# Mamba's D skip: from two matmuls a unit on TensorE to a multiplication and an addition on GpSimd

## The reference, cut to what matters

```
zxbcdt = x @ in_w
z, xBC, dt = split(zxbcdt);  dt = softplus(dt + dt_bias)
xBC = silu(causal 4-tap convolution of xBC)
xs (4 heads x 64), Bm (128), Cm (128) = split(xBC)
y = ssd(xs * dt, dt * A, Bm, Cm)          # chunked state-space scan
y = y + D_skip[head] * xs                 # the D skip
y = y * silu(z)                           # the gate
y = y * rsqrt(mean(y*y) + 1e-5) * norm_w
out = y @ out_w
```

## Time and profile before

| what | us |
|---|---|
| median of 3 runs | 2361.59 |
| the runs | 2361.59, 2362.1, 2351.86 |
| the profiled execution, its own time | 2355.98 |
| span of the profiled execution | 2354.0 |
| outside the span | 1.98 |
| PE busy in the span | 1775.5 (75%) |
| DVE busy | 1386.8 (59%) |
| POOL busy | 993.7 (42%) |
| ACT busy | 821.7 (35%) |

### The profile page before, as it was taken

The page is one execution under the profiler, slowest core; times in us unless marked ns, Lnnn a source line. Parts: engine busy times, 40 slices in busy tenths (PEclk is TensorE's granted clock), DMA queues, the critical chain, the costliest instruction groups (busy, mean ns, idle before and its releaser), DMA issues. The chain is left out here.

```text
span 2354.0 us, 38902 instructions
## 1 busy us (share of the span) xinstructions
PE 1775.5 (75%) x11182; PEld 1463.1 (62%) x11183; DVE 1386.8 (59%) x3442; ACT 821.7 (35%) x1791; POOL 993.7 (42%) x1144
## 2 busy tenths in 40 slices
PE   3979833799999999999588993277772897357673
PEld 3559731488888888888445883166661465247663
DVE  4445465688888888885544445733446344843435
ACT  1322212455555555554132221033331322034331
POOL 2017540376666666665201652155551001045552
PEclk9999955899999999999599995588895767578887
DMA  6001120000000000000400115011112001201114
GB/s 192 1 10 42 36 73 0 0 2 1 1 2 1 1 2 1 1 1 1 156 0 10 37 37 156 8 37 38 38 37 74 1 0 59 58 27 39 39 37 125
DMA packets 60844, 81.39 MB, mean 35 GB/s; under 512 B 24720, under 2 KB 30896, under 8 KB 60720
## 3 DMA queue, kind: packets, MB, share of 16 engines
q1 hardware_dynamic: 46640, 51.01, 7.0%
q0 software_dynamic: 14080, 28.86, 4.4%
HBM read 54.93 MB, written 24.90 MB: 34 GB/s over the span
## 5 line engine op out<-in xcount | busy, mean ns | idle before, releaser
L650 POOL DMA_INDIRECT rows_in<-xn_rows,slot_token x220 | 221.0, 1004 | 461.4 <-SPq L643 395.6
L696 PE MATMUL ps<-w,inner_slot 128*128 x1760 | 269.3, 299 | 92.5 <-DVE y L787 64.5
L656 POOL DMA_INDIRECT y_rows<-y,slot_row x220 | 224.6, 1021 | 246.2 <-DVE y L787 138.3
L684 PE MATMUL ps<-gT,w_slot 128*128 128x128 f32 x1760 | 270.0, 303 | 52.9 <-ACT gT L718 48.3
L696 PEld LDWEIGHTS ps<-w,inner_slot 128*128 128x128 f32 x1760 | 239.6, 210 | 110.1 <-issue 109.6
L684 PEld LDWEIGHTS ps<-gT,w_slot 128*128 128x128 f32 x1760 | 245.0, 215 | 64.9 <-issue 42.7
L764 DVE TENSOR_TENSOR hb<-ps,b 128x512 f32<-128x512 f32 x142 | 98.1, 691 | 274.0 <-PE ps L684 135.1
L1431 DVE SCALAR_TENSOR_TENSOR cv<-ps,cw,cv 128x1021 f32<-128x1021 f32 (+2 forms) x192 | 245.1, 1277 | 17.6 <-ACT cv L1369 15.1
L1529 POOL TENSOR_TENSOR y<-t,sz 128x256 f32<-128x256 f32 x128 | 94.5, 739 | 210.4 <-DVE t L1467 210.4
L1274 PE MATMUL ps<-xnT,win 128*128 128x512 f32 x256 | 132.2, 642 | 31.4 <-DVE cv L1431 26.9
L1325 PE MATMUL ps<-XB,M 128*128 128x64 f32 x1024 | 142.5, 262 | 0.0
(11 more groups left out here) (255 smaller groups left out, 4312.4 us busy)
## 6 DMA issues: line engine op xcount, KB each, us to landing
w<-in_L_ffn_W SPq DMA_DIRECT2D x6, 2048.0 KB, 11.3
back<-y_rows SPq DMA_DIRECT2D x48, 256.0 KB, 5.5
xn_rows<-xn SPq DMA_DIRECT2D x32, 256.0 KB, 3.6
rows_in<-xn_rows,slot_token POOLq DMA_INDIRECT x220
y_rows<-y,slot_row POOLq DMA_INDIRECT x220
out_x<-x SPq DMA_DIRECT2D x8, 256.0 KB, 3.1
win<-in_L_attn_in_w SPq DMA_DIRECT2D x1, 1544.0 KB, 9.5
b<-in_L_ffn_b SPq DMA_DIRECT2D x2, 512.0 KB, 10.9
```

The source lines that it names most:

```text
L650: nc.gpsimd.indirect_dma_start(k.rows_in[:, q, :], None, k.xn_rows[:, :], bass.IndirectOffsetOnAxis(ap=k.slot_token[:, s:s + 1], axis=0)). ...
L656: nc.gpsimd.indirect_dma_start(kept, bass.IndirectOffsetOnAxis(ap=k.slot_row[:, s:s + 1], axis=0), k.y[:, s % RING, :], None).then_inc(sto ...
L684: ins = nc.tensor.matmul(h1[:, u, b * P:(b + 1) * P], w[:, b * P:(b + 1) * P], k.gT[:, r, :], start=True, stop=True)
L696: ins = nc.tensor.matmul(py[:, q % 2, :], k.inner_slot[:, q % RING, b * P:(b + 1) * P], w_dn[:, ds(e * (FB * D) + b * D, D)], start=(b == ...
```

## The change

The two D skip matmuls of a unit go. POOL gets a new step, `skip`, behind `weigh`: it multiplies XB's x, which ACT has copied, by D for each head, into a new tile XD of two buffers. `gated` first adds t2 to XD, and then, behind a wait for that, multiplies the sum by the gated z. ACT's copy into XB now also waits for the `skip` of two units before, and DVE's t2 waits for the addition of two units before in place of the product. D is loaded once for all partitions by one DMA in place of two, and the eight instructions that made `diagD` are gone.

```diff
-        m.dsk, m.diagD = S("dsk", [P, ME * 2]), S("diagD", [P, ME * 2, P])
+        m.dtb, m.aneg, m.dsk = (S(n, [P, MEH]) for n in ("dtb", "aneg", "dsk"))
...
-        by_side = w["L0_attn_D_skip"].rearrange("e (b s) -> s (e b)", s=2)
-        for side in range(2):
-            loads.append((m.dsk[side * HD:(side + 1) * HD, :], by_side[side].unsqueeze(0).to_broadcast([HD, ME * 2])))
+        loads.append((m.dsk[:, :], w["L0_attn_D_skip"].rearrange("e h -> (e h)").unsqueeze(0).to_broadcast([P, MEH])))
...
-            for n in range(ME * 2):
-                do(V.tensor_scalar(m.diagD[:, n, :], k.ident[:, :], m.dsk[:, n:n + 1], None, ALU.mult))
...
+    XD = S("XD", [P, 2, ZW])
...
+                wait(pe, b["M"], u + 1)
                 for h in range(MH):
                     hd = slice(h * HD, (h + 1) * HD)
-                    if h % 2 == 0:
-                        blk = h // 2
-                        nc.tensor.matmul(bankY[:, blk * P:(blk + 1) * P], channels(pas, blk)[:, cols],
-                                         m.diagD[:, e * 2 + blk, :], start=True, stop=False, skip_group_check=True)
-                    if h == 0:
-                        wait(pe, b["M"], u + 1)
-                    ins = nc.tensor.matmul(bankY[:, hd], M[:, r, h * P:(h + 1) * P], XB[:, r, hd], start=False, stop=True,
-                                           skip_group_check=True)
+                    ins = nc.tensor.matmul(bankY[:, hd], M[:, r, h * P:(h + 1) * P], XB[:, r, hd], start=True, stop=True)
...
                 wait(act, b["y"], u - 1)
+                wait(act, b["XD"], u - 1)
                 inc(A.copy(XB[:, r, :], bankX[:, 0:ZW + P]), b["XB"])
...
                 wait(dve, t1_done, u + 1)
-                wait(dve, b["y2"], u - 1)
+                wait(dve, b["skipped"], u - 1)
...
+            def skip(u):
+                _, e, _, _ = unit(u)
+                wait(pool, b["y2"], u - 1)
+                inc(G.tensor_tensor(heads(XD[:, u % 2, :]), heads(XB[:, u % 2, 0:ZW]),
+                                    bcast(m.dsk[:, e * MH:(e + 1) * MH], 2, HD), ALU.mult), b["XD"])
...
-                inc(G.tensor_tensor(y2[:, u % 8, :], t2[:, u % 2, :], sz[:, u % 8, :], ALU.mult), b["y2"])
+                wait(pool, b["XD"], u + 1)
+                inc(G.tensor_tensor(XD[:, u % 2, :], XD[:, u % 2, :], t2[:, u % 2, :], ALU.add), b["skipped"])
+                wait(pool, b["skipped"], u + 1)
+                inc(G.tensor_tensor(y2[:, u % 8, :], XD[:, u % 2, :], sz[:, u % 8, :], ALU.mult), b["y2"])
...
                     weigh(t + OPEN)
+                    skip(t + OPEN)
```

More of the change, by code:

```diff
@@ L1015, in mamba @@
         m.cw, m.cb = S("cw", [P, ME * 4, TAPS]), S("cb", [P, ME * 4])
-        m.dtb, m.aneg = (S(n, [P, MEH]) for n in ("dtb", "aneg"))
-        m.dsk, m.diagD = S("dsk", [P, ME * 2]), S("diagD", [P, ME * 2, P])
+        m.dtb, m.aneg, m.dsk = (S(n, [P, MEH]) for n in ("dtb", "aneg", "dsk"))
         m.tri, m.identb = S("tri", [P, P]), S("identb", [P, P], BF16)
@@ L1227, in mamba_units @@
     a = {n: k.counter(f"piece_{n}") for n in names}
-    names = ("z", "z_tanh", "z_gate", "x_turned", "cb", "exponent", "XB", "L", "M", "Xw", "y", "s", "carried", "state",
+    names = ("z", "z_tanh", "z_gate", "x_turned", "cb", "exponent", "XB", "XD", "skipped", "L", "M", "Xw", "y", "s", "carried", "state",
              "t2", "y2", "squared", "yT_turned", "yT", "out", "added")
```

## The result

The changed kernel takes 2376.36 us in the median of 6 runs (2370.81 to 2379.99), the kernel before 2359.9 in the median of 6 (2351.86 to 2362.1). The ratio is 1.0072 with a 95% interval of 1.0052 to 1.0093: the change costs about 17 us. The forecast was 2372 us in a range of 2351 to 2395, and the time lies in it.

The account below looks back on a forecast made before the run. PE bounds the middle, with a ring of POOL, ACT and DVE 0.79 us a pair behind. The middle's +14.1 and the end's -3.3 give +10.8 us on the median of 2361.6: 2372 us, range 2351 to 2395.

Parts of the forecast that it names:

- The ring: Units stage: wait chain gated, silu_piece, ACT's tanh to L, DVE's M to t2, back to gated; 9.96 us a pair, 0.79 behind PE.
- plain pair: Even step and the odd one behind it, without `normalise`: 9.96 + 0.80 = 10.76 us, against 10.75 before.
- the count from E: Times in a pair counted from the end of DVE's even t2: `carried` ends at 4.51, odd t2 at 5.81, product at 7.76.
- `gated` grows by 0.80: On POOL: the addition takes 0.73 us and the product's semaphore wait some 0.07, lengthening `gated` by 0.80.
- `skip` is free: On POOL: `weigh` and `skip` end at about 5.7, just ahead of the odd t2's end at 5.81, costing nothing.
- A pair with `normalise`: Every second pair in the middle: POOL's queue delays `carried` and DVE's state, making it 11.14 us, 0.38 more.
- The sign that DVE's state would wait for `carried` in both kinds of step: Expected in the trace after: DVE's state waits for POOL's `carried` in even and odd steps; no size given.
- The end of the stage: Units 115 to 127: first units lose 1.8 us, the nine to unit 127 take 34.7 instead of 39.8; together -3.3 us.
- POOL's round: Behind unit 118: addition, product, `carried`, DVE's state to t2, 3.48 us a unit, or 4.95 with `normalise`; PE needs 4.01.
- The cover for the removed matmuls: In the middle: PE's work falls from 10.75 to 9.75 us a pair, but the ring is late next, so gain 0.
- the first rival: PE's saving comes through: pairs fall to the ring's 9.96 us, -46 with the end of the stage, 2316 us; chance 0.07.
- `diagD` and the load cost nothing: Ahead of the units: DVE's eight `diagD` instructions are hidden behind ACT's copy, and one DMA less counts 0.

## Why the prediction was right, point by point

- **The ring is close behind PE, and `gated` is in it.** Right. A plain pair takes 10.75 us (10.76 forecast, with the matmuls' 1.00 us gone), the anchors of the count from E lie within 0.02 us of their forecast, and moving silu ahead of `gated` takes the price away.
- **The ring's length of 9.96 us.** Right: 10.75 - 0.80 = 9.95. But the first pair doesn't show this ring "by itself", as I wrote: a second ring, through tap 2 and PE's projection, is there only 0.05 us behind it, and the pair keeps its 9.96 when silu is moved away. The forecast didn't suffer, since the addition lengthens the ring through silu alone.
- **`gated` grows by 0.80.** Right: addition 0.72 to 0.73, and the product starts 0.80 after it in even steps. In odd steps the product takes 1.06 beside `twice_sigmoid`, as `carried` did before. The Trainium skill's GPSIMD Engine Reference (Key points) lets GpSimd contend with VectorE instructions in a 2-port mode or with two SBUF inputs; in the trace after, the additions beside DVE's taps, which read PSUM, took 0.73 in even steps, so it agrees. Its doubled cost for two inputs (Engine selection), applied to DVE's t2 of 0.42, would have made the addition 0.84; the measured 0.73 decides.
- **`skip` is free.** Right by experiment in the middle: 624.48 against 624.42 us. "Three POOL operations" under "What comes" is a slip: two are new, `skip` and the addition, and the sum counts them so.
- **A pair with `normalise` takes 0.38 more.** Right in size (11.16 against 11.14 forecast, 0.41 more). By moving it, its place is shown for 7.7 of some 11.5 us (28 pairs of 0.41); the rest is put down to the addition that it holds up in its new place, which the rows above show for one pair. The sign that DVE's state would wait for `carried` in both kinds of step came true only here: in the plain pair the state of the even step (738.78) starts 1.2 us after `carried` has ended.
- **The end of the stage: -3.3 us forecast, +0.9 measured.** This is the step that failed. "Units 115 to 118 lose 1.8 us" measured 2.2. "The nine to unit 127 take 34.7" measured 38.5. I had compared PE's work per unit with POOL's round, and had left out a wait of PE that was hidden before: the turn of a unit waits for the `add` of the one before, which stands behind t2 on DVE. That closes a third ring of 3.87 us, hidden at PE's 4.51. With this wait out of the way the nine units take 35.05. Of the 3.8 us that they took too long, some 2.5 are this ring and 1.0 is the clock that fell in the last unit.
- **The cover for the removed matmuls.** I wrote that PE was 0.79 us a pair ahead of the ring. The kernel without any D skip shows that only 0.52 of it can be had: from the seventh unit on `add` stands between t2 and the taps, 0.27 us, and the ring through the taps and the projection, now 10.22, comes ahead of the one through silu. The forecast didn't rest on this, but the first rival's 2316 us did; what can be had in that order is 2330.
- **`diagD` and the load cost nothing.** Right: from SP's last loads of the layer ahead to PE's first projection for Mamba it took 388.39 - 299.96 = 88.43 us before and 392.75 - 304.30 = 88.45 after.
- **Clock.** PE fell to 92% busy in the middle, and its granted clock stayed at 1.00, that is 2.4 GHz. It fell to 0.50 only in the last unit, as said above; the sum had no term for it.

The size came out 5 to 6 us low on 10.8, about half of it the missed wait. The chances of "same" (0.47) and "slower" (0.44) were near each other since the sum lay on the line of 0.5%; the measured 0.7% lies just beyond it, on the side to which I had given the smaller chance.

## What to carry to other kernels

An engine that is busy all the time hides the rings of waits right behind it. Before work is taken from it, follow each ring once around, and look for it in a stretch where the busy engine has less to do. Such a stretch gives the length of the longest ring there, and hides the next one just as well: here two rings tied at 9.96 us, and moving one instruction showed the second. Work moved to an engine with idle time is free only in the right place: with the same POOL operations, unit 0 to 127 took 15.5 us longer than before in the old order (683.77 against 668.29), and 27 us less (641.12) when one independent instruction was put ahead of the one that waits.

## What the runs showed that I had not expected

The traces repeat far better than the totals: two kernels that differ by the order on POOL had the same 609.85 us for 57 pairs, while the totals of one kernel spread over 10 us and more. So for a change inside one stage, the time from one marked instruction to another told apart effects of 1 us, which the whole runs here could not.
